# Quantised feed-forward of a decoder: one third of the gate and of gate times up goes to GpSimd, and two maxima are taken in pieces

## What is computed

```python
def act_qdq(x):                       # 16 bits, one scale for the whole tensor
    scale = jnp.maximum(jnp.max(jnp.abs(x)) / qmax, 1e-12)
    return jnp.clip(jnp.round(x / scale), -qmax - 1.0, qmax) * scale

def fixed_qdq_u16(x):
    scale = 1.0 / 65536.0
    return jnp.clip(jnp.round(x / scale), 0.0, 65535.0) * scale

x = act_qdq(x)
up = act_qdq(x @ lpbq_dequant(w_up).T)
gate = act_qdq(x @ lpbq_dequant(w_gate).T)
sig = fixed_qdq_u16(jax.nn.sigmoid(gate))
gate = act_qdq(gate * sig)
o = act_qdq(gate * up)
return o @ lpbq_dequant(w_down).T
```

## Time and profile before

| | us |
|---|---|
| median of 3 runs | 919.0 (918.51 to 919.17) |
| the profiled execution | 912.8 |
| its span in the trace | 910.9 |

### The profile page before, as it was taken

The page is one execution under the profiler, slowest core; times in us unless marked ns, Lnnn a source line. Parts: engine busy times, 40 slices in busy tenths (PEclk is TensorE's granted clock), DMA queues, the critical chain, the costliest instruction groups (busy, mean ns, idle before and its releaser), DMA issues.

```text
span 910.9 us, 14508 instructions
## 1 busy us (share of the span) xinstructions
PE 856.6 (94%) x4558; PEld 561.4 (62%) x4578; DVE 662.2 (73%) x1175; ACT 572.5 (63%) x1080; POOL 307.3 (34%) x296
## 2 busy tenths in 40 slices
PE   8999999999899888989899879999999999999997
PEld 4576644776535543445545546776357888888884
DVE  3576626777779769659768766563368999999996
ACT  5356624665557556468677732334667888888886
POOL 0111004674038400019438526434001344444330
PEclk9999999999999998999999999999999999999999
DMA  9000000113000000000000061403009999999981
GB/s 358 25 1 0 0 1 18 38 50 118 0 1 2 1 1 0 1 0 2 2 0 2 2 259 52 139 24 99 1 29 217 239 245 240 244 241 244 239 222 60
DMA packets 28721, 77.82 MB, mean 85 GB/s; under 512 B 4432, under 2 KB 11856, under 8 KB 28208
## 3 DMA queue, kind: packets, MB, share of 16 engines
q1 hardware_dynamic: 27520, 74.74, 29.3%
q0 software_dynamic: 1152, 2.44, 0.8%
HBM read 72.50 MB, written 6.28 MB: 86 GB/s over the span
## 4 chain that ended last, share of the span: by engine, by line
PE 71%; DVE 16%; ACT 10%; issue 2%; DMA 1%; SPq 0%; POOL 0%; another core or an unknown queue 0%; DVEq 0%; ACTq 0%; POOLq 0%
PE ps L839 10%; PE ps L841 9%; PE ps L840 9%; PE ps L611 4%; PE ps L1228 4%; PE ps L601 3%; PE ps L624 3%; PE ps L291 2%; PE ps L1246 2%; ACT arena L1948 2%; PE ps L1550 2%; PE ps L228 2%; PE ps L1632 2%; PE ps L1603 1%; DVE arena L771 1%
## 5 line engine op out<-in xcount | busy, mean ns | idle before, releaser
L839 PE MATMUL ps<-parts 128*128 128x512 f32 x416 | 166.6, 401 | 4.0 <-DVE ps L2563 1.5
L841 PE MATMUL ps<-parts 128*128 128x512 f32 x416 | 162.1, 390 | 0.0
L840 PE MATMUL ps<-parts 128*128 128x512 f32 x416 | 161.9, 389 | 0.0
L869 ACT ACTIVATE parts<-ps 128x512 fp32r<-128x512 f32 x192 | 115.2, 600 | 54.1 <-PE ps L841 24.6
L873 DVE TENSOR_TENSOR parts<-ps,parts 128x512 fp32r<-128x512 f32 x192 | 132.5, 690 | 7.2 <-ACT parts L869 1.2
L857 POOL TENSOR_TENSOR parts<-ring,zeros 128x1024 fp32r<-128x1024 f32 (+2 forms) x36 | 51.1, 1419 | 183.1 <-PE ps L841 142.2
L2563 DVE TENSOR_TENSOR ps<-ps,arena 128x512 f32<-128x512 f32 x156 | 108.2, 694 | 3.0 <-DMA arena<-m_comb 2.1
L839 PEld LDWEIGHTS ps<-parts 128*128 128x128 f32 x416 | 78.2, 188 | 24.9 <-DVE parts L873 3.4
L2097 ACT ACTIVATE ps<-ps 128x512 f32<-128x512 f32 x156 | 90.8, 582 | 2.8 <-PE ps L841 0.4
L841 PEld LDWEIGHTS ps<-parts 128*128 128x128 f32 x416 | 78.1, 188 | 16.7
L840 PEld LDWEIGHTS ps<-parts 128*128 128x128 f32 x416 | 78.1, 188 | 16.0 <-issue 0.5
(11 more groups left out here) (479 smaller groups left out, 1535.7 us busy)
## 6 DMA issues: line engine op xcount, KB each, us to landing
arena<-m_comb SPq DMA_DIRECT2D x156, 256.0 KB, 4.7
ring<-m_in SPq DMA_DIRECT2D x20, 512.0 KB, 5.5
arena<-m_in SPq DMA_DIRECT2D x4, 1408.0 KB
pack<-pack_in SPq DMA_DIRECT2D x1, 2058.5 KB, 10.3
ring<-m_up_in SPq DMA_DIRECT2D x8, 256.0 KB, 2.7
slots_x<-empty_in SPq DMA_DIRECT2D x1, 1584.1 KB, 7.8
pack<-pack_in SPq DMA_DIRECT2D x1, 1187.0 KB, 14.8
pack<-pack_in SPq DMA_DIRECT2D x1, 1149.5 KB, 12.5
```

Of the source, the lines that this page charges most:

```text
L839: nc.tensor.matmul(dst, w_high, x_high, start=start, stop=False, skip_group_check=True)
L840: nc.tensor.matmul(dst, w_high, x_low, start=False, stop=False, skip_group_check=True)
L841: return nc.tensor.matmul(dst, w_low, x_high, start=False, stop=stop, skip_group_check=True)
L869: nc.scalar.activation(m_hh[0:rows, p], ps[0:rows, src, :], ACT.Copy).then_inc(R(t, "_hh"), 1)
```

## The change

Of the third third (c = 2) VectorE no longer does `bounded`, `gated` or the multiplication by up. GpSimd does them, with five instructions on 128 x 1024: bound and add 192, take 192 off, multiply by the gate; later, when the gate is rounded, take the rounding constant off and multiply by up. Each waits for the one before it by the semaphore `mid_pool`, which is the old `a_zeros` under a new name. The maxima of rounds 3 and 4 are taken in three instructions in place of one: the first two thirds at once (2048 columns), then, after a wait for GpSimd, the last third (`largest_third`), then the two results. ScalarE rounds the last third of the gate ahead of the middle one.

```diff
-            for c in range(1, 3):
+            for c in (2, 1):
                 A_(q_gate[:, c * T:(c + 1) * T], q_gate[:, c * T:(c + 1) * T], ACT.Identity, scale=q_i[:, 3:4], bias=round_up).then_inc(S("f1_sig"), 1)
...
+            def largest_third(buf, n):
+                dve.wait_ge(S("mid_pool"), n)
+                link(V.tensor_reduce(q_part[:, 0, 1:2], third(buf, 2), AX.X, ALU.max, apply_absolute_value=True))
...
             gated(1)
-            bounded(2)
-            gated(2)
-            largest(3, q_gate).then_inc(S("f1_col"), 1)
+            V.tensor_reduce(q_part[:, 0, 0:1], q_gate[:, 0:2 * T], AX.X, ALU.max, apply_absolute_value=True)
+            largest_third(q_gate, 4)
+            largest(3, q_part[:, 0, 0:2]).then_inc(S("f1_col"), 1)
...
             dve.wait_ge(S("f1_up_gate"), 18)
-            for c in range(3):
-                dve.wait_ge(S("f1_sig"), 3 + c)
+            for c in range(2):
+                dve.wait_ge(S("f1_sig"), 3 + 2 * c)
                 ins = V.scalar_tensor_tensor(out=third(q_up, c), in0=third(q_gate, c), scalar=ROUND, in1=third(q_up, c),
                                              op0=ALU.subtract, op1=ALU.mult)
             link(ins)
-            largest(4, q_up).then_inc(S("f1_col"), 1)
+            V.tensor_reduce(q_part[:, 0, 0:1], q_up[:, 0:2 * T], AX.X, ALU.max, apply_absolute_value=True)
+            largest_third(q_up, 6)
+            largest(4, q_part[:, 0, 0:2]).then_inc(S("f1_col"), 1)
...
             narrow_sums_gpsimd(pool, "x1")
+            pool.wait_ge(S("f1_sig"), 3)
+            G.tensor_scalar(q_sig[:, 2 * T:3 * T], q_sig[:, 2 * T:3 * T], 65535.0 / 65536.0, 192.0, ALU.min, ALU.add).then_inc(S("mid_pool"), 1)
+            pool.wait_ge(S("mid_pool"), 2)
+            G.tensor_scalar(q_sig[:, 2 * T:3 * T], q_sig[:, 2 * T:3 * T], 192.0, None, ALU.subtract).then_inc(S("mid_pool"), 1)
+            pool.wait_ge(S("mid_pool"), 3)
+            G.tensor_tensor(q_gate[:, 2 * T:3 * T], q_sig[:, 2 * T:3 * T], q_gate[:, 2 * T:3 * T], ALU.mult).then_inc(S("mid_pool"), 1)
+            pool.wait_ge(S("f1_sig"), 4)
+            pool.wait_ge(S("f1_up_gate"), 18)
+            G.tensor_scalar(q_gate[:, 2 * T:3 * T], q_gate[:, 2 * T:3 * T], ROUND, None, ALU.subtract).then_inc(S("mid_pool"), 1)
+            pool.wait_ge(S("mid_pool"), 5)
+            G.tensor_tensor(q_up[:, 2 * T:3 * T], q_gate[:, 2 * T:3 * T], q_up[:, 2 * T:3 * T], ALU.mult).then_inc(S("mid_pool"), 1)
             wait_x(pool, 6)
```

More of the change, by code:

```diff
@@ L694, in narrow_values_scalar @@
             waits(act, t)("_vproj", 1)
-            act.wait_ge(S("a_zeros"), 1)
+            act.wait_ge(S("mid_pool"), 1)
             for p in range(2):
@@ L2625, in _ @@
             pool.wait_ge(S("y_ready"), 6)
-            G.memset(a_vflat, 0.0).then_inc(S("a_zeros"), 1)
+            G.memset(a_vflat, 0.0).then_inc(S("mid_pool"), 1)
             narrow_sums_gpsimd(pool, "x1")
+            pool.wait_ge(S("f1_sig"), 3)
[9 more added lines that the diff above has]
+            G.tensor_tensor(q_up[:, 2 * T:3 * T], q_gate[:, 2 * T:3 * T], q_up[:, 2 * T:3 * T], ALU.mult).then_inc(S("mid_pool"), 1)
             wait_x(pool, 6)
```

## The result

The changed kernel takes 921.75 us (median of 20 runs, 918.78 to 925.89), the kernel before in the same comparison 919.17 (20 runs, 914.70 to 922.97). The ratio of the two kernels' runs is 1.0038 (that of their medians is 1.0028), with a 95% interval of 1.0025 to 1.0051: slower by 2.3 to 4.7 us, where I had forecast 0.6 us less and given "slower" 0.23. The time also lies outside the range of 917.2 to 921.4.

The account below looks back on a forecast made before the run. VectorE was taken to bound round 3, VectorE and TensorE's fills together round 4. Round 3 saves 0.75 us, round 4 nothing of its own, the fills pass 0.6: 919.0 - 0.6 = 918.4 us, range 917.2 to 921.4.

Parts of the forecast that it names:

- What bounds the kernel: VectorE alone sets the time to round 3's maximum at 354.72; round 4's is bound by VectorE and TensorE's fills together.
- What leaves VectorE: Round 3 loses 0.67 + 1.21 us, round 4 a 1.17 us product; each 3.35 us maximum becomes pieces totalling 3.67 plus gaps.
- What GpSimd needs: Round 3 on GpSimd: two TENSOR_SCALARs at 1.04 us each and a 2.40 product, ready at 350.5 if alone.
- Rival (b): GpSimd's TENSOR_SCALAR is dear: at 1.89 us, round 4 ends 1.9 us later, time 920.9; stops paying near 1.25; chance 0.17.
- What the two engines do to each other: VectorE and GpSimd: whoever comes second waits, then takes its own time less 0.15 us (GpSimd) or 0.20 (VectorE).
- the rounds by that count: With those waits, round 3's maximum ends 0.75 us earlier and round 4's 0.71 earlier, round 4 winning nothing of its own.
- The fills: TensorE's fills before round 5 begin 0.75 us earlier and let through 0.75 or about 0.4; 0.6 us taken.
- rival (c): TensorE's clock falls behind round 4 instead, 14 fills take 6.3 us for 3.19: +2.3 to +2.6, 921.4; chance 0.16.
- My bound of 2.3 us of idle time: TensorE's clock falls at the worse place once fills end more than some 2.3 us before VectorE.
- (a): The engines hinder each other little: round 3 gives 1.58 us, round 4 some 0.2 more; 917.2 to 918.1; chance 0.11.
- (d): GpSimd's first TENSOR_SCALAR needs its code loaded, some 6 us by the skill, time an estimate of 924; chance 0.03.
- Chances: For the whole kernel: faster 0.07, same 0.70, slower 0.23, with about 1.8 us as what a measurement can tell.

Follow-up runs that it names:

- the copies: The changed kernel with GpSimd's three TENSOR_SCALARs replaced by copies of the same 1024 columns; one execution timed, 919.4 us.
- the first of before: The kernel before, unchanged, in its first profiled execution, the trace the forecast was read from; median time 919.17 us.
- narrow share: The kernel before with round 3 alone changed, GpSimd taking only the last 256 columns of the gate; one execution timed, 916.6 us.
- round 3 only: The kernel before with only the change's half at round 3, round 4 and ScalarE's order as before; ratio 1.0007 to before.
- before again: The kernel before, unchanged, timed and traced a second time; ratio 0.9997 to before.
- pieces: The kernel before with only the maxima of rounds 3 and 4 taken in three instructions, all work on VectorE; ratio 1.0003 to before.
- round 4 only: The kernel before with only the change's half at round 4, round 3 as before; ratio 1.0011 to before.
- price only: The kernel before with each GpSimd instruction form run on a spare buffer in GpSimd's idle time; one execution timed, 921.5 us.
- hindrance only: The kernel before, GpSimd running the change's five instructions on a spare buffer at the same moments, nobody waiting; one execution timed, 922.5 us.
- more fills: The changed kernel with 44 and 41 TensorE fills in place of 22 and 24; ratio 1.0069 to before, 1.0044 when run again.

## Why the prediction was wrong

**What bounds the kernel**: right for round 3, and VectorE's stretches R3 and R4 are what moved, 2.44 and 0.85 us, and nothing else in the block but the clock. That the fills bind round 4 together with VectorE was true only of the trace that was read: in the second trace of the same kernel they ended 1.45 us ahead.

**What leaves VectorE**: right. The maxima took 2.29, 1.22 and 0.15 us as worked out, and cost 0.25 us a round where 0.38 was counted.

**What GpSimd needs**: this is the step that failed. I took a TENSOR_SCALAR for 1.04 us, the copy's row, "since a TENSOR_SCALAR reads one tensor as the copy does", and put the upper bound at 1.89, the nearest product. The prediction named 1.25 us as the price above which it would be wrong. It costs 3.64 us with two operations and 2.78 with one, both above the upper bound. The number of tensors read does not set its price; the trace of before held no row of the form, and both ends were rows of other instructions. By the forecast's own rule that three of them stand in the chain, the error is (3.64 - 1.04) + (2.78 - 1.04) = 4.34 us in round 3 and 1.74 in round 4. R3 came out only 3.19 over the forecast's 8.28, and R4 0.82 over its 7.70: the forecast has GpSimd wait for `bounded(1)`, `gated(1)` and the second product of round 4, and these were over while its long steps still ran. Rival (b) had the mechanism, and stopped short of the size: it gave 1.9 us later for both rounds, where 2.44 and 0.85 were measured, together 3.3. Its slope, 0.3 us for each 0.1 on a step, was too steep over this distance: 6.08 us more of price made R3 and R4 together 4.03 us longer than with the copies (19.99 for 15.96). Its time of 920.9 is 0.85 below the measured one. The Trainium skill's estimate that I set beside it (GPSIMD Engine Reference, "Elementwise — side-by-side cycle accounting"), 1.03 cycles an element for up to two operations, fits the copy (0.8 ns a column) and not the TENSOR_SCALAR (2.5 to 3.4 ns, 3 to 4 cycles at the 1.2 GHz it states). The measurement decides.

**What the two engines do to each other, and the rounds by that count**: right at the price assumed, shown by the copies, whose R3 and R4 came within 0.06 us. For the real instruction one part does not carry over: a TENSOR_SCALAR of GpSimd does not block for its whole length.

**The fills**: wrong twice. That they cut VectorE's saving to 0.6 us was read from one trace; with the copies, where VectorE did save 0.71 us in R3, they ended 2.84 us before TensorE's next real work and cut nothing, and in every other trace with the same number of fills but the first of before that pause was 1.0 us or more. And TensorE's part is no matter of tenths. In the 13 traces other than the first of before, the clock fell to 1.2 GHz during the 14 fills in seven; that costs 1.7 us, or 2.8 with the copies.

**The clock, rival (c)**: its mechanism is real, and it is not only a rival. It struck in the copies as described. In the change and in the second trace of before the clock fell at that place too, but behind round 3 as well. My bound of 2.3 us of idle time was wrong: it fell behind 1.30 us (narrow share), 1.38 (round 3 only), 1.45 (before again) and 1.58 (pieces) and stayed up behind 1.00 (round 4 only), 1.18 (price only) and 1.48 (hindrance only). The length of that one pause does not decide it alone. How much of the 2.3 to 4.7 us measured it makes is open: R3 and R4 alone come to 3.3, near the middle of the interval, and the 14 fills were long in the second trace of before as well.

**(a)** is refuted (`bounded(1)` and `gated(1)` took 1.20 and 1.67 us in the copies, for 0.67 and 1.21), **(d)** too (first and second call alike).

**Chances**: slower at 0.23 rested on a range for the one unseen price that was too narrow.

## What to carry to other kernels

Before elementwise work is moved to another engine, measure the very instruction there, with its number of operations; a copy of the same size says nothing about it, and if no row has it, the upper bound must lie well above the nearest ones (here 3.64 us, against rows of 1.04 and 1.89). Work on a chain with waits between its steps is only worth moving if the receiver's whole chain, at measured prices, ends before the giver would ask: in round 3 VectorE gave up 1.9 us of work and GpSimd took 8.8 for it (3.64 + 2.78 + 2.35). And compare stretches inside the trace, not spans: two profiled executions of one kernel differed by 8.0 us, and stretches as short as R3 agreed to 0.01.

## What the runs showed of the hardware that I had not expected

- GpSimd's TENSOR_SCALAR on 128 x 1024 float32 is dearer than its product of two tensors: 3.64 us with min and add, 2.78 with a subtraction, against 2.35 for the product of two tensors in the change (1.89 alone with the same tensor as both inputs) and 1.04 for a copy.
- It hinders VectorE for a part of its length only. In the change it could begin when `gated(0)` ended at 344.23; `bounded(1)`, due at 344.47, took 0.53 us more than its 0.67, and `gated(1)` ran unhindered from 345.97 to 347.18 while it went on to 347.73. In the trace with the hindrance alone, `bounded(2)` was held again near its end (1.06 for 0.69). In the narrow share, `bounded(1)` began 0.24 us after GpSimd could begin its step of 256 columns, and kept its 0.67 us. A copy and a product held VectorE to their end: with the copies, one ended at 350.26 and `gated(1)`, due at 349.66, at 351.33; in price only, a product ended at 328.41 and L2368, due at 326.70, at 328.96 (2.26 us for 0.76). Which access is held when is not settled by these runs. The Trainium skill (SBUF — State Buffer, "SBUF: two separate sides") has the pair locked "for the whole instruction"; the copy and the product agree, TENSOR_SCALAR does not.
- Keeping TensorE's clock up in the block shortened the block by 2 us and the time by nothing that could be measured, in two comparisons. Outside, the last block took 242.7 and 247.1 us with more fills and 241.5 in the change, but also 244.1 in price only, which has no more fills than before. Its matmuls run beside transfers that keep the DMA engines over 0.9 busy, but what lengthened it was not followed up, and it is open.
